# A nearest-neighbour graph convolution: marks of a pair by one ScalarE instruction, and the first bfloat16 piece of the features cast by GpSimd

## The reference, cut to what matters

```python
x_flat = x.reshape(B, C, N).transpose(0, 2, 1)        # x: group-normed input
emb = einsum('bnc,ec->bne', x_flat, dist_w)
d2 = sq[:, :, None] + sq[:, None, :] - 2.0 * einsum('bne,bme->bnm', emb, emb)
_, idx = top_k(-sqrt(clip(d2, 0)), 24)
adj = (mask_of(idx) & (dist <= 10)) | eye(N)
X_lin = x_flat @ fc_w.T + fc_b                        # the features
S = (adj / De[:, None, :]) @ adj.T / Dv[:, :, None]   # De, Dv: column and row sums
out = S @ X_lin + x_flat
o = batchnorm(out) * gamma + beta
return x + o * sigmoid(o)
```

## Time and profile before

| | value |
|---|---|
| profiled execution, its own time | 183.22 us |
| its span (first to last instruction) | 181.4 us |
| runs | 183.22, 183.35, 187.37 us |
| TensorE matmul busy | 154.6 us (85%) |
| VectorE busy | 147.5 us (81%) |
| ScalarE busy | 116.5 us (64%) |
| GpSimd busy | 78.4 us (43%) |
| ScalarE: marks, L645 | 32 instructions, 9.5 us |
| ScalarE: cast to the first piece, L615 | 8 instructions, 5.1 us |

### The profile page before, as it was taken

How to read it: one execution, slowest core, us unless ns; L and a number is a source line. 1 busy time by engine, 2 the same in 40 slices (tenths; PEclk the granted TensorE clock), 3 DMA queues, 4 the chain that set the end, 5 groups by cost and what they waited for, 6 DMA issues and landing times.

```text
span 181.4 us, 4108 instructions
## 1 busy us (share of the span) xinstructions
PE 154.6 (85%) x1257; PEld 100.4 (55%) x1257; DVE 147.5 (81%) x888; ACT 116.5 (64%) x221; POOL 78.4 (43%) x96
## 2 busy tenths in 40 slices
PE   7688999978997999599999999999967999999000
PEld 2223533344465872366668646866737888989000
DVE  0667999989999969996969489695998984499783
ACT  2145759999969987995556989355864443090190
POOL 1002209606895481095342858471526156650100
PEclk9999999999999999999999999999996999999855
DMA  6811000071522923065514225591509457700057
GB/s 186 284 66 2 2 0 4 1 91 29 121 64 52 92 59 86 3 120 120 116 29 94 58 62 84 150 90 31 116 0 92 88 155 81 175 5 0 0 185 280
DMA packets 41483, 14.84 MB, mean 82 GB/s; under 512 B 38736, under 2 KB 39656, under 8 KB 41456
## 3 DMA queue, kind: packets, MB, share of 16 engines
q1 hardware_dynamic: 40592, 14.14, 37.8%
q10 hardware_dynamic: 864, 0.40, 0.8%
HBM read 4.02 MB, written 2.13 MB: 34 GB/s over the span
## 4 chain that ended last, share of the span: by engine, by line
PE 57%; ACT 18%; DVE 11%; issue 7%; DMA 2%; POOL 1%; ACTq 0%; DVEq 0%; POOLq 0%
PE pt L442 21%; PE pg L412 15%; PE po L469 13%; ACT key L625 5%; ACT H L634 4%; PE po L375 3%; ACT left L575 3%; DVE cand L864 2%; DMA x_sb<-x 2%; DVE xn L1079 2%; PE po L399 2%; ACT xn L709 1%; DVE t L958 1%; PE po L386 1%; ACT right L581 1%
## 5 line engine op out<-in xcount | busy, mean ns | idle before, releaser
L864 DVE MAX8 cand<-key 128x8 f32<-128x64 f32 x512 | 80.9, 210 | 1.5 <-ACT key L625 1.2
L442 PEld LDWEIGHTS pt<-xp,H 128*128 128x128 bf16 x768 | 45.5, 99 | 18.2 <-issue 15.9
L442 PE MATMUL pt<-xp,H 128*128 128x128 bf16 (+1 forms) x768 | 50.0, 223 | 2.7 <-DVEq L924 2.7
L625 ACT ACTIVATE key<-pg 128x512 f32<-128x512 f32 x64 | 34.5, 590 | 21.3 <-PE pg L412 21.0
L412 PE MATMUL pg<-right,left 64*128 64x512 f32 x128 | 41.6, 641 | 5.3 <-ACT key L625 4.5
L756 POOL CAST wide<-HT 128x1024 fp32r<-128x1024 bf16 x31 | 31.5, 1040 | 28.6 <-PE po L469 20.2
L634 ACT ACTIVATE H<-key,bound 128x1024 bf16<-128x1024 f32 x32 | 36.7, 1146 | 9.5 <-DVE bound L902 6.8
L469 PE MATMUL po<-wide,tp 128*128 128x512 f32 x96 | 25.5, 409 | 2.2 <-ACT tp L653 2.2
L412 PEld LDWEIGHTS pg<-right,left 64*128 64x128 f32 x128 | 12.7, 184 | 16.6 <-ACT key L625 8.6
L469 PEld LDWEIGHTS po<-wide,tp 128*128 128x128 f32 x96 | 17.6, 193 | 5.8 <-issue 2.4
L734 POOL TENSOR_TENSOR xr<-x,xp 128x512 f32<-128x512 f32 x8 | 9.0, 1126 | 22.1 <-ACT xp L615 22.1
(11 more groups left out here) (96 smaller groups left out, 169.9 us busy)
## 6 DMA issues: line engine op xcount, KB each, us to landing
dvb<-inv_rows SPq DMA_DIRECT2D x3, 512.0 KB, 4.2
out<-xn SPq DMA_DIRECT2D x6, 256.0 KB, 2.2
x_sb<-x SPq DMA_DIRECT2D x1, 1024.0 KB, 6.0
x_sb<-x SPq DMA_DIRECT2D x1, 512.0 KB, 3.5
HT<-H SPq DMA_TRANSPOSE x32, 2.8
out<-xn SPq DMA_DIRECT2D x4, 128.0 KB, 2.2
x_sb<-x ACTq DMA_DIRECT2D x1, 256.0 KB, 3.1
x_sb<-x SPq DMA_DIRECT2D x1, 256.0 KB, 3.5
```

The lines of the kernel that those rows point to most:

```text
L442: mm = pe.matmul(pt[:, j // T_BLOCKS, at:at + wide], lhs, x_cols(b, t, q, wide), start=(t == 0 and j % T_BLOCKS == 0 and q == 0), stop=(t ...
L625: act.activation(key[:, k % KEYS, cols], pg[:, h, :], ACT.Copy).then_inc(s["drained"], 1)
L864: ins = dve.max(cand[:, k % 2, c, :], key[:, k % KEYS, c * CHUNK:(c + 1) * CHUNK])
```

## The change

The cast of the features to their first bfloat16 piece moves from ScalarE (`drain_x`) to GpSimd (ahead of the residue in `x_middle`), with its wait for a free buffer of `xp`; it has a semaphore of its own, `x_cast`, and `x_hi` now counts one event for each half. `mark` does nothing for the first tile of a pair, and for the tail it makes the marks of the whole group in one instruction; the flag's matmul waits for the group's count.

```diff
--- before.py
+++ after.py
@@ -175,7 +175,7 @@
 
         names = ("const_in d_in w_in x_in0 x_in1 x_in23 out_done setup ones_cols gstat gmean gdm gvar gsd gscale "
                  "xn0_ready xn_ready filled drained po_filled po_drained e_sq n_filled l_made r_made norm_out "
-                 "x_hi x_res x_mid "
+                 "x_hi x_cast x_res x_mid "
                  "x_lo limited signed marked flagged flag_read noise_made key_used h_ready h_used bank_summed t_scaled t_hi "
                  "t_lo widened widened_last gvar_in bn_var rdv_ready turned inv_copied rdv_out dvb_in spread dvb_made o_ready o_used y_ready step slow_step stats_done bn_sd "
                  "bn_affine silu_done summed filler_set").split()
@@ -417,7 +417,7 @@
                     return
                 i = TAIL_OF[k]
                 n = len(GROUPS[i])
-                pe.wait_ge(s["marked"], k + 1)
+                pe.wait_ge(s["marked"], i + 1)
                 if i >= FLAGS:
                     pe.wait_ge(s["flag_read"], i - FLAGS + 1)
                 a = GROUPS[i][0] % THRS
@@ -607,13 +607,9 @@
                     act.wait_ge(s["filled"], 2 * pair["x", b, 0] + h + 1)
                 if b > 0:
                     act.wait_ge(s["x_lo"], 2 * (b - 1) + h + 1)
-                if b >= XBUFS:
-                    act.wait_ge(s["h_used"], TILES * (b - XBUFS + 1))
                 act.activation(x32[:, cols], x_bank(b, h), ACT.Copy).then_inc(s["x_hi"], 1)
-                act.wait_ge(s["x_hi"], 4 * b + 2 * h + 1)
+                act.wait_ge(s["x_hi"], 2 * b + h + 1)
                 act.sem_inc(s["po_drained" if ("x", b) in po_pair else "drained"], 1)
-                act.activation(x_cols(b, slice(h * TH, (h + 1) * TH), 0),
-                               x32[:, cols].rearrange("p (t c) -> p t c", c=C), ACT.Copy).then_inc(s["x_hi"], 1)
 
             def drain_key(b, t):
                 p = pair["key", b, t]
@@ -636,13 +632,17 @@
 
             def mark(k):
 
-                b, t = divmod(k, TILES)
+                if k not in TAIL_OF:
+                    return
+                g = GROUPS[TAIL_OF[k]]
+                b, t = divmod(g[0], TILES)
+                at = g[0] % THRS
                 act.wait_ge(s["signed"], k + 1)
-                if k == 0:
+                if g[0] == 0:
                     act.wait_ge(s["setup"], 5)
                 if k >= THRS:
                     act.wait_ge(s["flagged"], [k - THRS in g for g in GROUPS].index(True) + 1)
-                act.activation(marks[:, k % THRS:k % THRS + 1], cs[:, b, t:t + 1], ACT.Sigmoid, scale=-STEEP,
+                act.activation(marks[:, at:at + len(g)], cs[:, b, t:t + len(g)], ACT.Sigmoid, scale=-STEEP,
                                bias=most[:, :]).then_inc(s["marked"], 1)
 
             def t_high(b):
@@ -730,7 +730,11 @@
 
             def x_middle(b, h):
 
-                pool.wait_ge(s["x_hi"], 4 * b + 2 * h + 2)
+                pool.wait_ge(s["x_hi"], 2 * b + h + 1)
+                if b >= XBUFS:
+                    pool.wait_ge(s["h_used"], TILES * (b - XBUFS + 1))
+                pool.tensor_copy(x_piece(b, h, 0), x_tiles(x32, h)).then_inc(s["x_cast"], 1)
+                pool.wait_ge(s["x_cast"], 2 * b + h + 1)
                 pool.tensor_tensor(x_tiles(xr32, h), x_tiles(x32, h), x_piece(b, h, 0), ALU.subtract)\
                     .then_inc(s["x_res"], 1)
                 pool.wait_ge(s["x_res"], 2 * b + h + 1)
```

## The result

Twenty runs of the changed kernel have a median of 182.06 us (179.85 to 184.41), twenty of the kernel before 184.95 us (183.14 to 188.74). The ratio is 0.9837, 95% interval 0.9801 to 0.9873: 1.6% less time, clear of zero and less than 2%. It leaves out the slow runs, those more than 1.5% above the fastest of their kernel (eight of the changed kernel's twenty, four of the other's). The medians of all runs differ by 2.9 us, the lowest times, 183.14 and 179.85, by 3.3. Runs of both kernels lie on levels, the changed kernel's near 179.9, 182.0, 182.9 and 184.3. The experiments show that drops of TensorE's clock make most of the steps between them, and that the gain is there without any such drop.

What follows compares the result with a forecast made beforehand. ScalarE was taken to bound the kernel until about 44 us, then mostly TensorE. Gains of 2.4 + 0.3 + 0.3 = 3.0 us, taken from 183.35, gave 180.3 us, range 178.5 to 182.3.

Steps and rivals of the forecast that it cites:

- 2.4 for the early stretch: Up to TensorE's second scatter: casts and marks removed ahead of it on ScalarE make that scatter start 2.4 us earlier.
- 0.3 at the gather: TensorE's stall at 76.97 us, before the first gather: mark 12 in its chain goes, giving 0.3 us.
- 0.3 at image 3: Key fill at 99.64 us: without the first-half cast, the copy of image 3's second half starts earlier, giving 0.3 us.
- GpSimd at nothing: Eight added casts on GpSimd, 0.61 us each, cost nothing on the path; tightest cover is image 1's noise before tile 8's threshold.
- (a): VectorE becomes the bound early, in 24 to 47 us: only 1.4 us won, 181.8 us; chance 0.12.
- (b): More is won: marks worth 0.33, second-half cast and mark 6 count too; 4.1 us gain, 179.1 us; chance 0.12.
- second-half cast and mark 6: ScalarE's cast of image 1's second half and tile 6's mark, taken as off the path, would also count.
- (d): Slower: clock drops at the stalls of 57.28 and 76.97, 2.8 us lost each; 2.6 us slower, 185.8 us; chance 0.05.
- (e): Casts win nothing because the copy's wait is unchanged; only marks count, 1.2 us gain, 182.0 us; chance 0.05.
- (c): TensorE's clock: drop at 137 us gone (178.8 us, chance 0.08) or a second at 77 us (181.6 us, chance 0.08).
- another low digit: Sign against the forecast: a further low value in the profile's row of TensorE's granted clock.

Runs made afterwards that it cites:

- off-path kernel: Kernel before with all fillers, plus only three casts moved to GpSimd and nine mark pairs merged, those called off the path: median 182.67 us, against 182.79.
- path-only kernel: Kernel before with only three casts moved to GpSimd (image 0, image 1's first half) and four mark pairs merged: median 181.31 us, ratio 0.9817.
- kernel with four casts: Changed kernel with each of GpSimd's new casts made four times, 24 more casts: median 182.02 us, ratio to the kernel before 0.9858.
- the casts alone: Kernel before with all fillers, plus only the eight casts moved to GpSimd: median 180.84 us; measured way 99.97 us, 1.89 less.
- fillers in the later stalls: Changed kernel plus matmuls whose result nothing reads, in TensorE's stalls before the first gather and tile 24's scatter: median 179.95 us, ratio 0.9743.
- its twelve with fillers: Twelve runs of the kernel before with all fillers added: 182.52 to 183.27 us, median 182.79, ratio to the kernel before 0.9902.
- marks only: Kernel before with only the marks of a pair merged, all eight casts still on ScalarE, no unread matmuls added: median 183.6 us, ratio 0.9926.
- casts only: Kernel before with only the eight casts moved to GpSimd, every mark by itself, no unread matmuls added: median 182.87 us, ratio 0.9905.
- left moved: Changed kernel with ScalarE's second half of left behind the key copy at steps 3, 8 and 13: median 182.54 us, ratio 0.9857.
- all fillers: Unread matmuls in TensorE's two later stalls, plus seven more before 16 us; on the changed kernel: median 179.90 us, ratio 0.9739.

## Why the prediction was right

**The bound.** ScalarE's queue led until the second scatter and TensorE after it: confirmed by the off-path kernel (0.1 us for 4.3 us of relief) and the path-only kernel (18.47 for 18.46).

**The two prices.** A cast was taken at 0.54 and measured 1.07 for two. A mark was taken at 0.30 between bounds of 0.20 and 0.33, and was worth the upper bound, 0.33: the next instruction starts 0.09 behind the accumulator read's start. The 0.19 that the prediction worked out from the Trainium skill ("ScalarE: Activation LUTs", What ACT_TABLE_LOAD costs) is what a mark takes between starts, and there it agrees (29.21 to 29.41). It is not what the removal of one gives, since the mark also started 0.13 later than 0.09 behind the read.

**2.4 for the early stretch** was 2.55. The difference is small: the first scatter is 1.70 earlier for 1.64, by the marks' 0.03 each, and the key fill behind it takes 1.31 to the second scatter, for about 1.4. **0.3 at the gather** was 0.32. **0.3 at image 3** was 0.37. The sum was 3.0, the measured way 3.28; the ratio of the runs, 0.9837, put on the 183.35 that the forecast started from, gives 180.4 against 180.3. That this is closer than 3.0 is to 3.28 is luck: the ratio holds how often the runs of either kernel fell on which level.

**GpSimd at nothing** held, also with four times the casts. The noise ended at 52.26 against a threshold at 54.76, a cover of 2.5 us, and 48.0 against 50.41, 2.4, was the forecast. ScalarE's waits for `pg` rose from 21.0 to 27.8 us, of which 2.1 belong to the early clock drop; "about 5" was forecast.

**The rivals.** (a), VectorE as the bound early, came nowhere near: its new wait of 1.68 us in the kernel with four casts cost nothing. (b) was half right on one price, the mark's 0.33, and wrong on the second-half cast and mark 6. (d) did not come: no trace has a drop behind the stall of 1.09, and the one at the gather cost 1.5 to 1.6 and not 2.8. (e) fell by the casts alone, 1.89.

**Where I misjudged: (c), the clock.** I gave a second drop at the gather's stall a chance of 0.08, because the one trace had none there. Three traces of the experiments show it. Of the changed kernel's twenty runs nine lie near 182.0, 2.2 above the lowest level, and with fillers in the later stalls no run does. The drop accounts for 1.5 to 1.6 of these 2.2; the step of 0.5 in the start would make most of the rest, but no trace of such a run of the changed kernel was taken. The kernel before has eleven of its twenty runs between 184.35 and 185.32, 1.2 to 2.2 above its lowest, and none of its twelve with fillers lies above 183.27. So the drop was very likely part of the base and not a danger of the change, though no trace shows it in the kernel before itself.

It cancelled in the ratio, but the absolute time did not: 183.35 was the median of three runs, two of them on the lowest level, and twenty gave 184.95. The predicted 180.3 lies between the lowest level and the measured median of 182.06, and that median lies only 0.24 under the top of the range. By its own list the forecast would have been wrong if the clock row showed another low digit. It showed one, in slices 4 to 6, ahead of everything that was changed; the sign did not tell a drop that the change brings from one that the base has too.

## What to carry to other kernels

Where two engines are both near full, ask by how much one lags the other at the same tile, and price an edit in starts of neighbours, not in durations: 8.2 us taken off an engine were worth 3.3, and which 3.3 could be told instruction by instruction. Check with the complement too, the edits that should be worth nothing. And look at more than one execution's clock before an absolute time is forecast: behind a stall of 2 us three of six traces lost 1.5 us more. Fillers in it held the clock, and they cost nothing that shows where they ended before the wait did (98.57 us with them, 98.56 without).

## What the runs showed of the hardware

- Behind TensorE's stall before the first gather, 1.9 to 2.2 us, the granted clock fell to 0.50 in three traces (marks only, casts only, path only) and held in three (before, changed, four casts), and it held in the one with left moved, where the stall was 3.45. The gather's first eight matmuls took 2.95, 3.46 and 3.49 us for 2.09, and the measured way was 1.5 to 1.6 us longer than with the clock held (101.46 for 99.97, 102.05 for 100.44).
- The early drop, in the changed kernel's trace 10 us at 0.50 and 4.1 to 4.2 us lost, came behind idle pieces of only 0.8, 0.8 and 0.3 us. The trace of the kernel before has the same pieces and no drop. Without fillers four of twenty runs of the kernel before and five of twenty of the changed one were 4 us or more above the lowest; with seven fillers in these pieces none of the 37 runs of the kernels that had all fillers was.
- With all fillers all runs of a kernel lie within 0.8 us of each other; without them ten runs of the kernel before lay within 6.0 (183.06 to 189.06).
- The Trainium skill ("TensorE: Matmul & The Clock Gate", What's actually happening) says that activity releases the throttle and idle time brings it back, observed free of the kernel's own timing. The end of the levels with fillers agrees with the first, and one stall with and without a drop behind it with the second.
